# Attention over the heads of a token: scores of token pairs, and probabilities transposed by VectorE onto a zeroed diagonal

## The reference

```python
Q = (q @ Wq.T + bq).reshape(bs, sl, H, HD)      # q: layernorm(x)
K = (k @ Wk.T + bk).reshape(bs, sl, H, HD)      # k, v: the context
V = (v @ Wv.T + bv).reshape(bs, sl, H, HD)
score = jnp.einsum('bshd,bsgd->bshg', Q, K)
weight = jax.nn.softmax(score, axis=-1)
attn = jnp.einsum('bshg,bsgd->bshd', weight, V).reshape(bs, sl, nf)
x = x + attn @ Wo.T + bo
x = x + ffn(layernorm(x))                        # 8 experts, 2 for a token, and a shared one
```

## Time and profile before

| | us |
|---|---|
| median of 3 runs | 1491.42 (1491.32 to 1495.39) |
| the profiled execution | 1494.03 |
| its span, first to last instruction | 1492.3 |
| TensorE busy in the span | 1404.3 (94%) |
| VectorE busy | 911.3 (61%) |
| ScalarE busy | 647.1 (43%) |
| GpSimd busy | 503.7 (34%) |

### The profile page before, as it was taken

The page is one execution under the profiler, slowest core; times in us unless marked ns, Lnnn a source line. Parts: engine busy times, 40 slices in busy tenths (PEclk is TensorE's granted clock), DMA queues, the critical chain, the costliest instruction groups (busy, mean ns, idle before and its releaser), DMA issues.

```text
span 1492.3 us, 33015 instructions
## 1 busy us (share of the span) xinstructions
PE 1404.3 (94%) x10387; PEld 1070.7 (72%) x10388; DVE 911.3 (61%) x1984; ACT 647.1 (43%) x1500; POOL 503.7 (34%) x607
## 2 busy tenths in 40 slices
PE   4899999999999999689899999999999999999997
PEld 4788888888888888557576756666666666666674
DVE  6888888888888887848765632222222222224666
ACT  6355555566665666532153523333333333332221
POOL 4444444444444442200567301111111111114554
PEclk9899999999999999789999999999999999999999
DMA  5556666666667886746855342222222222226996
GB/s 193 135 128 174 175 176 177 177 173 175 176 176 176 182 190 169 249 181 258 142 86 71 79 143 71 78 84 84 84 79 84 84 77 84 84 71 214 310 311 223
DMA packets 261893, 223.20 MB, mean 150 GB/s; under 512 B 182997, under 2 KB 191261, under 8 KB 261486
## 3 DMA queue, kind: packets, MB, share of 16 engines
q1 hardware_dynamic: 241224, 178.62, 42.9%
q0 software_dynamic: 12880, 35.47, 7.8%
q10 hardware_dynamic: 7734, 8.40, 1.9%
HBM read 129.30 MB, written 67.96 MB: 132 GB/s over the span
## 4 chain that ended last, share of the span: by engine, by line
PE 81%; DVE 8%; ACT 4%; issue 2%; DMA 2%; SPq 1%; POOL 1%; another core or an unknown queue 0%; DVEq 0%; POOLq 0%; ACTq 0%
PE psum_b L728 43%; PE psum_a L728 32%; PE psum_b L1044 2%; PE psum_a L825 2%; PE psum_b L1066 2%; ACT spread_t L1112 1%; DVE d_m L1728 1%; SPq L488 1%; PE psum_b L754 1%; DMA heads<-in_wk_t 1%; DVE wdn L1814 1%; DVE gate_act L1703 1%; ACT z_parts L1148 1%; DMA wgu_in<-base_rows 1%; PE psum_b L786 0%
## 5 line engine op out<-in xcount | busy, mean ns | idle before, releaser
L728 PE MATMUL psum_a<-wgu,zg_t 128*128 x1704 | 268.9, 315 | 1.9 <-DVE zg_t L1825 1.7
L1980 POOL TENSOR_TENSOR spread<-pr,own 128x512 f32<-128x512 f32 x128 | 136.7, 1099 | 302.9 <-DVE pr L1480 291.9
L728 PEld LDWEIGHTS psum_a<-wgu,zg_t 128*128 128x128 f16 x1704 | 167.3, 98 | 90.1 <-issue 10.1
L2054 POOL DMA_INDIRECT zg<-z_rows,gather_ix x71 | 67.2, 946 | 412.6 <-DVE gather_ix L1821 405.3
L728 PE MATMUL psum_a<-zt_in,wsgu 128*128 128x256 f16 x1536 | 170.6, 273 | 2.1 <-DVE wsgu L1509 1.3
L728 PEld LDWEIGHTS psum_a<-zt_in,wsgu 128*128 128x128 f16 x1536 | 148.9, 98 | 25.9 <-issue 7.6
L1830 DVE SCALAR_TENSOR_TENSOR silu<-psum_a,w_scale,silu 128x352 f32<-128x352 f32 x71 | 41.5, 584 | 194.9 <-ACT silu L1319 194.9
L728 PE MATMUL psum_b<-wsdn,sh_t 128*128 128x512 f16 (+1 forms) x576 | 135.6, 390 | 16.7 <-DVE sh_t L1709 16.2
L728 PE MATMUL psum_b<-wdn,act_t 128*128 (+1 forms) x639 | 149.6, 379 | 1.6 <-DVE act_t L1837 1.6
L1319 ACT ACTIVATE silu<-psum_a,w_scale 128x352 f32<-128x352 f32 x71 | 39.3, 553 | 203.7 <-PE psum_a L728 203.7
L728 PEld LDWEIGHTS psum_b<-wsdn,sh_t 128*128 128x128 f16 (+1 forms) x576 | 54.8, 99 | 91.8 <-issue 19.7
(11 more groups left out here) (247 smaller groups left out, 2516.5 us busy)
## 6 DMA issues: line engine op xcount, KB each, us to landing
expert_rows<-y_sb SPq DMA_DIRECT2D x71, 256.0 KB
k_st<-k_parts SPq DMA_DIRECT2D x192, 64.0 KB, 2.1
q_st<-q_parts SPq DMA_DIRECT2D x180, 64.0 KB, 2.1
wgu_in<-in_wgu_t SPq DMA_DIRECT2D x8, 1408.0 KB, 17.4
x_sb<-in_x SPq DMA_DIRECT2D x16, 512.0 KB, 3.5
cx_in<-in_ctx_t SPq DMA_DIRECT2D x16, 512.0 KB, 7.1
x_res<-in_x SPq DMA_DIRECT2D x16, 512.0 KB, 5.5
value_rows<-heads SPq DMA_DIRECT2D x16, 512.0 KB, 7.0
```

The costliest lines, as they stand in the source:

```text
L728: return nc.tensor.matmul(o, l, r, start=start, stop=stop)
L1980: G.tensor_tensor(spread[:, u * UG:(u + 1) * UG, :].rearrange("p r (g t) -> p r g t", t=GT), pr[:, s, u * UG:(u + 1) * UG, :].unsqueeze(3) ...
L2054: pool.indirect_dma_start(out=zg[:, b, :], out_offset=None, in_=z_d[:, :], in_offset=bass.IndirectOffsetOnAxis(ap=gather_ix[:, b:b + 1], a ...
```

## The change

Tokens are no longer grouped by eight neighbours. A half of 128 tokens is cut in four strips b of 32 tokens (NB32 = 4), one for each quadrant of partitions, and a strip in 16 pairs of tokens (t = 0, 1) that lie 16 apart. The rows of one score matmul are 16 heads x 2 tokens = 32, and so are its columns: 64 matmuls of 32x32 a half, each into the quadrant of its strip, all in one bank. Two mask rows are left of eight, and the maximum runs over 2 tokens. q_st and k_st are laid out anew; a row's operands for a matmul lie 32 bytes apart, before 8.

The block diagonal of a group of 8 tokens (4 strips x 2) has in rows of strip b only columns of strip b. So spread_t is set to zero once (GpSimd), and each pass VectorE writes only what lies on the diagonal: it multiplies the exponentials with own_inv (the inverse sum where row and column have the same token, else zero) into a dense 128x512, and transposes it in 32x32 blocks, one instruction for each strip and half, straight into spread_t: eight instructions, each 32 partitions x 512 elements, written as pairs of floats 32 bytes apart. TensorE's 32 transposes, ScalarE's eight copies and GpSimd's eight products are gone.

The tokens of a group now lie 16 apart, so the copies of the sums write single floats 64 bytes apart into at_raw; before they wrote runs of 8. The values are written with heads in the order of their rows, and each of the 16 transfers that fetch them goes to 16 partitions. ScalarE reads queries and keys from PSUM without a permutation. TensorE's order has the scores of a half in one piece, each behind a half of the key projection; the first scores of the next pass are no longer at the end of a pass. On VectorE normalise_out comes before weigh_piece, and both halves' shifts before the first half's softmax. On GpSimd the square roots wait for nothing but their statistics.

```diff
-ROWS = 3 * HD + GT
-GI = 4
-NJ = BT // (GT * GI)
+PAIR = 2
+NB32 = P // HD
+ROWS = 3 * HD + PAIR
+NJ = BT // (PAIR * NG)
...
-SCORES = [(f"S{s}{u}", f"A{u}") for s in range(SUB) for u in range(NU)]
-TURN_W = [[(f"T{s}{u}", f"A{u}") for u in range(NU)] for s in range(SUB)]
-FULL_PASS = (AHEAD + SCORES + AHEAD_KQ + OUT + TURN_W[0] + AHEAD_V + BEHIND + TURN_W[1] + ROUTE
+SCORES = [(f"S{s}", f"A{s}") for s in range(SUB)]
+FULL_PASS = (AHEAD + SCORES + AHEAD_KQ + OUT + AHEAD_V + BEHIND + ROUTE
...
-        spread = sb("spread", [P, NG, P], F32, one)
+        paired = sb("paired", [P, 2, SUB, NG * H * PAIR], F32, one)
+        spread = paired[:, 0]
         spread_t = sb("spread_t", [P, SUB, NG * P], F32, one)
...
-                dst = at_raw[:, :, s * P:(s + 1) * P].rearrange("p c (j q t) -> p q c j t", q=GI, t=GT)[:, q]
+                dst = at_raw[:, :, s * P:(s + 1) * P].rearrange("p c (t j q) -> p q c j t", q=4, t=GT)[:, q]
...
-                src = v_d[bass.ds(i * BT, BT), :].rearrange("(n t) (c l d) -> l c t n d", t=GT, c=KC, l=4)
-                for l in range(4):
-                    for c in range(KC):
-                        at = (l * KC + c) * GT
-                        sp.dma_start(v_p[at:at + GT, :, :], src[l, c]).then_inc(v_moved, 16)
+                src = v_d[bass.ds(i * BT, BT), :].rearrange("(s t g) (h d) -> s t h g d", s=SUB, t=GT, h=H)
+                for s in range(SUB):
+                    for t in range(GT):
+                        at = t // PAIR * HD + t % PAIR
+                        sp.dma_start(v_p[at:at + HD - t % PAIR:PAIR, s * NG:(s + 1) * NG, :], src[s, t]).then_inc(v_moved, 16)
...
-            def scores(s, i, us):
-
-                for u in us:
-                    step = f"S{s}{u}"
-                    o = bank_ap(step)
-                    wait_free(pe, step, i)
-                    if s == 0 and u == 3 and not (isinstance(i, int) and i == 0):
-                        pe.wait_ge(half_out, i)
-                    if s == 0 and u == 0:
-                        pe.wait_ge(k_moved, (i + 1) * (3 * 4 * 16))
-                        pe.wait_ge(q_moved, (i + 1) * (3 * 4 * 16))
-                    for g in range(UG):
-                        n = s * NG + u * UG + g
-                        last = mm(o[:, g * P:(g + 1) * P], q_st[:, n // GI, :, n % GI], k_st[:, n // GI, :, n % GI], True, True)
-                    last.then_inc(full[BANK_OF[step]], 1)
-
-            def transpose_weights(s, i):
-                for u in range(NU):
-                    step = f"T{s}{u}"
-                    wait_free(pe, step, i)
-                    pe.wait_ge(spread_ready, i * (SUB * NU) + (s * NU + u + 1))
-                    for g in range(UG):
-                        last = nc.tensor.transpose(bank_ap(step)[:, g * P:(g + 1) * P], spread[:, u * UG + g, :], ident[:, :])
-                    last.then_inc(full[BANK_OF[step]], 1)
+            def scores(s, i):
+
+                step = f"S{s}"
+                wait_free(pe, step, i)
+                if s == 0:
+                    pe.wait_ge(k_moved, (i + 1) * (3 * 4 * 16))
+                    pe.wait_ge(q_moved, (i + 1) * (3 * 4 * 16))
+                for g in range(NG):
+                    for b in range(NB32):
+                        q_side, k_side = (st[:, s * NB32 + b].rearrange("p h (t g) -> p (h t) g", g=NG)[:, :, g] for st in (q_st, k_st))
+                        last = mm(bank_ap(step)[HD * b:HD * (b + 1), g * HD:(g + 1) * HD], q_side, k_side, True, True)
+                last.then_inc(full[BANK_OF[step]], 1)
 
             def attend(s, i):
 
                 step = f"P{s}"
                 wait_free(pe, step, i)
+                pe.wait_ge(spread_out, i * SUB + (s + 1))
                 if s == 0:
-                    for u in range(NU):
-                        wait_drained(pe, f"T1{u}", i)
-                    pe.wait_ge(v_moved, (i + 1) * (H * 16))
+                    pe.wait_ge(v_moved, (i + 1) * (SUB * GT * 16))
+                elif not (isinstance(i, int) and i == 0):
+                    pe.wait_ge(half_out, i)
...
-                scores(0, i, (1,))
                 if ahead:
                     project_k(i, (0, 1))
-                scores(0, i, (2,))
+                scores(0, i)
                 if ahead:
-                    project_k(i, (2,))
-                scores(0, i, (3,))
-                scores(1, i, (0,))
+                    project_k(i, (2, 3))
+                scores(1, i)
                 if ahead:
-                    project_k(i, (3,))
-                scores(1, i, (1,))
-                if ahead:
-                    project_q(i, (0,))
-                scores(1, i, (2,))
-                if ahead:
-                    project_q(i, (1,))
-                scores(1, i, (3,))
-                if ahead:
-                    project_q(i, (2, 3))
+                    project_q(i, range(KC))
                 if behind:
                     project_out(0, i)
                     project_out(1, i)
-                transpose_weights(0, i)
                 if ahead:
                     project_v(i)
                 if behind:
                     turn_z(i)
...
-                transpose_weights(1, i)
...
-                    src = bank_ap(step)[:, c * BT:(c + 1) * BT].rearrange("p (j q t) -> p j t q", j=NJ, q=GI)
-                    nc.scalar.activation(whole_[:, 2 * b + c, :].rearrange("p (j t q) -> p j t q", j=NJ, q=GI), src, ACT.Identity,
+                    src = bank_ap(step)[:, c * BT:(c + 1) * BT]
+                    nc.scalar.activation(whole_[:, 2 * b + c, :], src, ACT.Identity,
                                          bias=bias[:, 2 * b + c:2 * b + c + 1], scale=scale)
-                    last = nc.scalar.activation(parts[:, HI, :, 2 * b + c, :].rearrange("p j (t q) -> p j t q", q=GI), src, ACT.Identity,
+                    last = nc.scalar.activation(parts[:, HI, :, 2 * b + c, :], src.rearrange("p (j t) -> p j t", j=NJ), ACT.Identity,
...
-            def weights_out(s, i):
-                for u in range(NU):
-                    step = f"T{s}{u}"
-                    wait_full(act, step, i)
-                    copy(spread_t[:, s, u * BANK:(u + 1) * BANK], bank_ap(step)).then_inc(drained[BANK_OF[step]], 1)
...
-            def own_scores(i, s, us):
-
-                for u in us:
-                    step = f"S{s}{u}"
-                    wait_full(dve, step, i)
-                    ins = V.tensor_reduce(out=sc[:, s, u * UG:(u + 1) * UG, :],
-                                          in_=bank_ap(step).rearrange("p (r g t) -> p r g t", r=UG, t=GT), axis=X, op=ALU.max)
-                    ins.then_inc(drained[BANK_OF[step]], 1)
+            def own_scores(i, s):
+
+                step = f"S{s}"
+                wait_full(dve, step, i)
+                V.tensor_reduce(out=sc[:, s].rearrange("p g h -> p (g h)"), in_=bank_ap(step).rearrange("p (r t) -> p r t", t=PAIR),
+                                axis=X, op=ALU.max).then_inc(drained[BANK_OF[step]], 1)
 
             def shift(i, s):
 
-                for u in range(NU):
-                    wait_drained(dve, f"S{s}{u}", i)
+                wait_drained(dve, f"S{s}", i)
                 link(V.tensor_reduce(out=row_max[:, s, :], in_=sc[:, s], axis=X, op=ALU.max))
...
-                V.tensor_tensor(pr[:, s], ex[:, s], row_inv[:, s, :].unsqueeze(2).broadcast_to([P, NG, H]), ALU.mult).then_inc(pr_ready, 1)
+                link(V.tensor_tensor(own_inv[:, s], row_inv[:, s, :].unsqueeze(2).broadcast_to([P, NG, PAIR]),
+                                     own[:, :].unsqueeze(1).broadcast_to([P, NG, PAIR]), ALU.mult))
+                link(V.tensor_tensor(spread[:, s].rearrange("p (g h t) -> p g h t", g=NG, t=PAIR), ex[:, s].unsqueeze(3).broadcast_to([P, NG, H, PAIR]),
+                                     own_inv[:, s].unsqueeze(2).broadcast_to([P, NG, H, PAIR]), ALU.mult))
+                if isinstance(i, int) and i == 0:
+                    dve.wait_ge(spread_zeroed, 1)
+                else:
+                    wait_full(dve, f"P{s}", i - 1)
+                placed = spread_t[:, s].rearrange("p (r b t) -> p b r t", b=NB32, t=PAIR)
+                for b in range(NB32):
+                    last = V.transpose(placed[HD * b:HD * (b + 1), b], spread[HD * b:HD * (b + 1), s].rearrange("p (r t) -> p r t", t=PAIR))
+                last.then_inc(spread_out, 1)
...
-                own_scores(i, 0, range(2))
                 next_key_scale(i - 1)
                 if ahead:
                     x_low(i)
-                own_scores(i, 0, range(2, NU))
+                own_scores(i, 0)
...
-                own_scores(i, 1, range(2))
+                own_scores(i, 1)
+                shift(i, 1)
                 softmax(i, 0)
-                own_scores(i, 1, range(2, NU))
-                shift(i, 1)
...
                     add_attended(i)
+                if behind:
+                    normalise_out(i)
                 if weighs:
```

(22 more changed lines are left out.)

43 lines of the change are left out of this document (20 added, 23 removed).

## The result

| | median us | span of the profiled execution | ratio to before, 95% interval |
|---|---|---|---|
| before | 1491.62 | 1492.3 | |
| after | 1586.54 (1582.86 to 1588.9) | 1581.1 | 1.0628 (1.0601 to 1.0655) |

The change makes the kernel 6.3% slower; 1493 us, and a range up to 1522, were forecast.

What follows compares the result with a forecast made beforehand. TensorE bounds the pass now; VectorE was to become the bound at 36.7 us a pass against 36.33. Over 13 passes +5 us, less 2.5 and 0.7 at the ends, about +2 on 1491.42: 1493 us, range 1481 to 1522.

Steps and rivals of the forecast that it cites:

- TensorE did stop being the bound: TensorE in a steady pass: its own work falls from 36.33 to 32.5 us, below VectorE's.
- 64 scores: TensorE's new score matmuls: 29 ns each, 3.8 us for the 128 of a pass.
- The transposes: VectorE's eight 32x512 transposes a pass: 0.69 us each, 5.5 us in all.
- The low parts of the queries: VectorE beside GpSimd: 792 ns against 682 for the keys; GpSimd's products vanish, giving back 0.2 us a pass.
- Rival (a): Strided copies of attended sums: 1.6 us a pass, 1514 us, up to 1530 if score matmuls pay too; chance 0.27.
- Rival (b): TensorE's clock falls around the turned z, keys before first scores take 1.4 us longer: 1514 us; chance 0.08.
- What else moves, at nothing: Attend's wait, moves, fetches, GpSimd's zeroing, ScalarE's reads and the values' write: all change without cost to the pass.
- 36.0 us, whatever the engines do: SP's (SyncE's) queue of fetches, moves and stores: its own round per pass, below VectorE's 36.7 us.
- some 8 us: Attend's wait for spread_out: VectorE has that much work after the last transpose before TensorE can get there.
- cover for GpSimd's roots: VectorE's order: weigh_piece (1.67 us), now behind normalise_out, no longer covers GpSimd's square roots, +0.2 us a pass.
- VectorE's round: VectorE's work and waits in a steady pass: from 34.66 to 36.7 us, making it the bound.
- the other waits and the tails behind them: VectorE's waits for ScalarE at z_parts, with tails behind waits: about 0.9 us a pass given back.

Runs made afterwards that it cites:

- e9: The changed kernel with a tail timing fetch issues, transposes and copies on idle engines; 1637 us in one execution, longer by the tail and compared with nothing.
- e10: The kernel before, with only the values' fetch in the changed kernel's shape (16 partitions, stride of two): 1550.3 us, ratio 1.039, pass 41.5 us.
- e4: The changed kernel with weigh_piece moved behind the second z_low: 1564.1 us, ratio 1.048, pass 41.4 us.
- e3: The changed kernel with attend's matmuls put ahead of the turned z and the router: 1563.8 us, ratio 1.048, pass 41.4 us.
- e5: The kernel before, with only the copies into at_raw writing one float in every 64 bytes: 1531.6 us, ratio 1.023, pass 39.2 us.
- e1: The changed kernel with at_raw written in runs of 8 floats again: 1552.1 us, ratio 1.040, pass 41.3 us.
- e2: The changed kernel with idle matmuls added on TensorE ahead of the turned z and the router: 1576.8 us, ratio 1.057, pass 42.3 us.
- e7: e6 with the values' fetch shaped as in the kernel before (values in wrong rows): 1516.8 us, ratio 1.014, pass 37.7 us.
- c1: Same computation as the changed kernel: old token order, eight larger fetch transfers, attend first, weigh_piece late; 1516.5 us, ratio 1.012, pass 37.9 us.
- c3: c1 with the 128x512 product moved to GpSimd and the transposes later in VectorE's order: 1512.9 us, ratio 1.011, pass 37.5 us.
- e6: The changed kernel with the edits of e1, e3 and e4 together: 1560.7 us, ratio 1.043, pass 41.4 us.

## Why the prediction was wrong

**Which row was read rightly.** TensorE did stop being the bound: 64 scores take 1.3 us (20 ns each; 29 assumed). The transposes stand at 0.72 with their gaps (0.69 forecast). The low parts of the queries fell from 792 to 687 ns and the subtraction of the second half from 0.78 to 0.43 us, as GpSimd left (rows 6). Both signs named for rivals (a) and (b) came: copies at 386 and 383 ns, a granted clock of 0.85.

**"What else moves, at nothing" failed, twice.**
- *"The moves themselves (24) and the fetches (16) keep number and bytes; a fetch goes to 16 partitions instead of 8."* They do, yet an issue takes SyncE 0.58 us instead of 0.28, for the stride over partitions (e9). This is 4.9 us a pass in a queue whose round the prediction itself had at "36.0 us, whatever the engines do". e10 measures what follows from that premise: 41.5 us, +58 us. The prediction had the bound and didn't add the issue to it. It also had that round too short: 36.0 came from two fetches 36.16 us apart, one of the shortest distances; over nine passes they lie 36.6 apart, so this queue was already falling behind TensorE's 36.33 and had nothing to spare.
- *Attend has "some 8 us" to spare.* For spread_out there was time: TensorE never waited for it in the steady passes. But attend stands behind the router, and the router waits for a bank that z_low(0) frees; the new order puts weigh_piece and the values ahead of z_low(0) (e4: 22 us; e3, by passing attend ahead: 23 us). The text looked at weigh_piece only as cover for GpSimd's roots.

**Rival (a) was the right mechanism, undersized, and a rival instead of a term.** The price per copy was right for VectorE (0.10 forecast, 0.09 measured) and low for ScalarE (0.12). Its worth was put at 22 us; in the kernel before it is 35 (e5), since there ScalarE's copies free the banks of TensorE's next scores and hold up VectorE's way to z, and in the changed one 34 (e1). The score matmuls, which read at 32 bytes, took 20 ns each and show no such price.

**Rival (b) too.** TensorE's clock fell around the turned z, but the loss is mainly in attend (3.64 against 1.95 us) and not in the keys, which ran at full pace until e3 moved attend. e2 gives 10 us for half of it.

**VectorE's round was 1 us short.** With strides, fetch and order put right it is 37.7 to 37.9 us (e7, c1) against 36.7. In e7 the second z and its wait for GpSimd are as in the changed kernel (1.24 and 0.77 us), and one wait is new:

```profile
289.32 0.69 DVE L1375 TENSOR_TENSOR k_parts<-heads,k_parts 128x512 f16<-128x512 f32 x1 [0.68 <-ACT k_parts L1095]
```

The second z takes 1.24 us instead of 0.55, since it now lies beside GpSimd's split of the context (+0.7; c3 shows the same beside GpSimd's product). VectorE waits for ScalarE's second copy of the keys (+0.7; nothing in the prediction). The transposes are dearer (+0.3). The wait for GpSimd's root grew from 0.46 to 0.77, 0.1 more than was allowed. Against these 1.8 us the other waits and the tails behind them gave back about 1.5 instead of 0.9, and some small terms 0.2. With nothing else wrong the change would have cost what e7 and c1 cost, some 20 us.

**Why the sum was so far off.** The terms do not add: strides 34, order 22 or 23, fetch nothing, each undone alone, but 70 together. Three rounds (VectorE's 37.7, SyncE's 41.4 to 41.5, the ring's 43.35) lay above the old 36.33, and only the longest shows. e1, e3, e4, e6 and e10 have the same pass within 0.2 us and yet lie between 1550 and 1564 us. Much of this is in the last pass: the last fetch starts within some 6 us in all of them (668.1 in e10 to 674.2 in e4), but the first matmul of the next stage's count starts at 741.8 in e10, 745.7 in e1, 750.4 in e6, 751.5 in e3 and 754.4 in e4. In e3 and e6 TensorE waits there once for the values, 21.4 and 19.9 us, as attend stands there ahead of the turned z and the router; in e1, where it stands behind both, the wait for the values is 1.7 us. What holds e4 back stays open. And the clock's own share is bounded, not measured.

## What to carry to other kernels

Work out the round of every queue as a sum, that of the DMA issuer among them, and price each issue by its new shape, since number and bytes don't say it. For every instruction moved, list what waits behind it in its own queue and which bank it frees: a 1.7 us reduction placed ahead of one release cost about 22 us. Take a queue's round from many passes and not from one pair. When undoing one part brings little, undo it together with the others before calling it harmless, and when several different edits stop at the same pass, look for the bound they have in common.

## What the runs showed of the hardware

- A DMA issue on SyncE to partitions with a stride (2 or 16) takes about 0.6 us, to adjacent ones 0.3 to 0.5; doubling its pieces of 128 bytes from 16 to 32 adds at most 0.05 us (e9). So few, larger transfers are cheap: c1 fetches the same bytes in 6.05 us instead of 12.2.
- Writing one float in 64 bytes of SBUF costs a 32x128 copy 0.09 us on VectorE and 0.12 on ScalarE; reading PSUM with that stride costs VectorE nothing (e9). The prices are those of the changed kernel against e1 (383 and 291 ns, 387 and 268).
- 64 matmuls of 98 rows, 32 columns, into 32 partitions take 1.28 to 1.36 us, 20 to 21 ns each, which is closer than the 25 ns the prediction cites from the Trainium skill ("TensorE: Matmul & The Clock Gate", Wait — 56ns, not 53.3ns?). That they go to four different groups of partitions in turn may be why; no run tells it.
- A tensor_scalar of 128x512 on VectorE took 0.55 us alone and 1.24 beside GpSimd. In the changed kernel the second z runs from 292.23 to 293.47, and GpSimd's cast of the context lies under it:

```profile
292.13 1.05 POOL L1932 CAST cx_t<-cx_in 128x1024 fp32r<-128x1024 f32 x1
```

  The z ends 0.29 us after the cast, as if about half of it had waited for the cast's end. The Trainium skill ("SBUF — State Buffer", SBUF: two separate sides) states that VectorE's two-port modes and GpSimd hold a shared pair of ports as an exclusive lock, for the whole instruction. The row agrees with a lock in that the z ends only behind the cast; a z that had waited for all of it would have ended 0.55 us behind it, and no row tells whether this z ran in such a mode. Where an operation comes to lie beside GpSimd is therefore a term of the sum, which the prediction counted only in the direction of a gain.
